# Attention on one core: the four column groups of the output moved within SBUF by SyncE and added by GpSimd, in place of eight matmuls and a VectorE copy

## The reference

```
q = (h @ Wq).reshape(Bb, Ss, H, Dh)
k = (h @ Wk).reshape(Bb, Ss, H, Dh)
v = (h @ Wv).reshape(Bb, Ss, H, Dh)
scores = jnp.einsum('bqhd,bkhd->bhqk', q, k) / jnp.sqrt(jnp.float32(Dh))
attn = jax.nn.softmax(scores, axis=-1)
ctx = jnp.einsum('bhqk,bkhd->bqhd', attn, v).reshape(Bb, Ss, Dd)
x = x + ctx @ Wo
```

## Time and profile before

| | |
|---|---|
| median of 3 runs | 3923.48 us (3914.27 to 3926.55) |
| span of the profiled execution | 3920.8 us, one core, mean granted clock 0.937 |
| PE busy | 3528.2 us (90%) |
| DVE busy | 2914.5 us (74%) |
| ACT busy | 2613.0 us (67%) |
| POOL busy | 696.1 us (18%) |

### The profile page before, as it was taken

One profiled execution on the slowest core, in us unless ns is written; L12 is line 12 of the kernel. 1 busy time (PEld: TensorE's weight loads), 2 busy tenths in 40 slices (PEclk: granted clock), 3 DMA queues, 4 the chain that ended last, 5 costly groups with the idle time before them and its releaser, 6 DMA issues. The chain is left out here.

```text
span 3920.8 us, 87382 instructions
## 1 busy us (share of the span) xinstructions
PE 3528.2 (90%) x29108; PEld 1918.7 (49%) x29108; DVE 2914.5 (74%) x5522; ACT 2613.0 (67%) x3037; POOL 696.1 (18%) x703
## 2 busy tenths in 40 slices
PE   8477999999999999999999999999999706999990
PEld 4243444444444444444444444444444605999980
DVE  1636999999999999999999999999996522333335
ACT  2132888888888888888888888888888103555540
POOL 0000000000000000000000000000000357888856
PEclk8595999999999999999999999999999757999995
DMA  3242010101101011010101101011000623444424
GB/s 95 81 161 51 12 25 14 24 13 26 24 13 26 13 24 25 13 24 13 26 16 21 26 12 25 14 24 25 14 12 7 204 102 126 146 136 138 142 83 133
DMA packets 158897, 206.66 MB, mean 53 GB/s; under 512 B 50064, under 2 KB 123664, under 8 KB 153232
## 3 DMA queue, kind: packets, MB, share of 16 engines
q1 hardware_dynamic: 140128, 173.78, 16.5%
q0 software_dynamic: 6336, 16.79, 1.4%
q10 hardware_dynamic: 12144, 12.06, 0.9%
HBM read 134.59 MB, written 66.85 MB: 51 GB/s over the span
## 5 line engine op out<-in xcount | busy, mean ns | idle before, releaser
L742 ACT ACTIVATE probs<-s_ps 128x1024 f32<-128x1024 f32 x2048 | 2056.1, 1026 | 408.6 <-PE s_ps L661 380.2
L776 DVE TENSOR_REDUCE unit_max<-m_ps 128x1 f32<-128x512 f32 x3584 | 2250.1, 686 | 57.1 <-PE m_ps L653 56.9
L676 PE MATMUL o_ps<-probs,v_here 128*32 128x256 f32 (+1 forms) x15360 | 1282.8, 406 | 0.5 <-ACT probs L742 0.5
L661 PE MATMUL s_ps<-q_stage,k_ring 50*128 50x512 f32 x4096 | 1024.4, 493 | 0.5
L653 PE MATMUL m_ps<-k_ring,q_stage 48*128 48x512 f32 x3840 | 963.6, 421 | 46.8 <-DMA q_stage<-qs_dram 25.9
L661 PEld LDWEIGHTS s_ps<-q_stage,k_ring 50*128 50x128 f32 x4096 | 384.2, 184 | 765.1 <-issue 646.2
L653 PEld LDWEIGHTS m_ps<-k_ring,q_stage 48*128 48x128 f32 x3840 | 619.9, 187 | 163.6 <-DVE unit_max L776 134.1
L676 PEld LDWEIGHTS o_ps<-probs,v_here 128*32 128x32 f32 x15360 | 303.2, 108 | 505.7 <-issue 502.7
L597 POOL TENSOR_TENSOR neg_max<-no_max,tile_max 128x4 f32<-128x4 f32 x127 | 25.3, 199 | 2447.9 <-DVE tile_max L791 2447.9
L1509 DVE TENSOR_TENSOR hidden_low<-h_ps,hidden_high 128x512 fp32r<-128x512 f32 x184 | 127.3, 692 | 366.4 <-ACT hidden_high L1473 366.4
L1469 ACT ACTIVATE h_ps<-h_ps,b_here 128x512 f32<-128x512 f32 x184 | 121.4, 660 | 255.4 <-PE h_ps L1406 255.4
(11 more groups left out here) (184 smaller groups left out, 2433.2 us busy)
## 6 DMA issues: line engine op xcount, KB each, us to landing
w_in<-in_W SPq DMA_DIRECT2D x46, 1024.0 KB, 4.9
q_stage<-max_turned SPq DMA_DIRECT2D x2048, 0.5 KB
q_stage<-qs_dram SPq DMA_DIRECT2D x768, 32.0 KB, 1.9
k_ring<-ks_dram SPq DMA_DIRECT2D x96, 128.0 KB, 4.3
slots_dram<-zero_rows SPq DMA_DIRECT2D x24, 512.0 KB, 6.7
rows_e<-slots_dram SPq DMA_DIRECT2D x24, 512.0 KB, 3.9
y_slots_dram<-y_out ACTq DMA_DIRECT2D x23, 512.0 KB, 4.3
qs_dram<-parts SPq DMA_DIRECT2D x16, 512.0 KB, 2.7
```

What stands on the lines that cost most here:

```text
L661: last = nc.tensor.matmul(s_ps[:, t % 2, k, :], k_ring[at:at + AROWS, par, P * t:P * t + P], q_stage[at:at + AROWS, buf * CHUNK:buf * CHUN ...
L676: last = nc.tensor.matmul(o_ps[at:at + SQ, lo:hi], v_here[:, par, first_tile(t) + 2 * k, :], probs[:, t, k, lo:hi], start=(pair == 0), sto ...
L742: nc.scalar.activation(probs[:, t, :, :], s_ps[:, t % 2, :, :], ACT.Exp).then_inc(exp_done, 1)
L776: nc.vector.tensor_reduce(unit_max[:, b, qt, 2 * j + k:2 * j + k + 1], m_ps[:, block_of(t, k) % 3, :], AX.X, ALU.max).then_inc(m_read, 1 + ...
```

## The change

`gather`, its making, `turn_o` and `copy_ctx` are gone. SP gets `align`: once `o_here` of chunk n is copied, it moves the three upper groups (17 partitions x 512 columns) with three transfers within SBUF to partitions 0 to 16 of `o_groups`. POOL gets `sum_o`: when all three have landed and the last store has read `ctx_stage`, it adds the four groups in three adds of 17x512 into `ctx_stage`, now 17x512 and single. SP's `store` is two transfers in place of five, one chunk later than before. In a chunk SP does `store(i - 2)` and then `align(i - 1)`, behind `rows(i + 1)` and `load_head`. POOL's list alternates `split_max(i + 2)` and `sum_o(i)`. ACT's `copy_o` also waits until the sum before last is done. The place of `turn_o` in the order of `m_ps` stays empty: DVE counts it off with the pair of slot 10, and PE's `block_of` is as it was.

```
@@ -470,7 +470,6 @@
         k_ring = sb("k_ring", [TOP_ROW + AROWS, 2, SIDE], F32R)
...
-        gather = sb("gather", [P, SQ])
@@ -480,14 +479,14 @@
...
         max_turned = sb("max_turned", [P, MROWS, SQ])
         o_here = sb("o_here", [P, CHUNK])
-        ctx_stage = sb("ctx_stage", [P, 2, P])
+        o_groups = sb("o_groups", [O_COLS, P // SQ - 1, CHUNK])
+        ctx_stage = sb("ctx_stage", [O_COLS, CHUNK])
@@ -527,21 +526,26 @@
...
-            def store(n, b, h, qc):
-                sp.wait_ge(m_read, n * RING_BLOCKS + ((LEAD + 1) * RING_BLOCKS + TURN_BLOCK + 1))
-                for t in range(TPC):
-                    sp.dma_start(dram["ctx"][ds(qc, 1), ds(h, 1), :, P * t:P * t + P].rearrange("a b c x -> (a b c) x"),
-                                 ctx_stage[SQ * t:SQ * t + DH, b, :]).then_inc(ctx_out[b], 16)
-                sp.dma_start(dram["z"][ds(h * CHUNKS + qc, 1), :].rearrange("a (t x) -> (a t) x", t=TPC),
-                             ctx_stage[DH:P:SQ, b, :]).then_inc(ctx_out[b], 16)
-
+            def align(n):
+
+                sp.wait_ge(o_copied, n + 1)
+                for g in range(1, P // SQ):
+                    sp.dma_start(o_groups[:, g - 1, :], o_here[SQ * g:SQ * g + O_COLS, :]).then_inc(o_aligned, 16)
+
+            def store(n, h, qc):
+                sp.wait_ge(o_summed, n + 2)
+                sp.dma_start(dram["ctx"][ds(qc, 1), ds(h, 1), :, :].rearrange("a b c x -> (a b c) x"),
+                             ctx_stage[0:DH, :]).then_inc(ctx_out, 16)
+                sp.dma_start(dram["z"][ds(h * CHUNKS + qc, 1), :], ctx_stage[DH:O_COLS, :]).then_inc(ctx_out, 16)
+
+            sp.sem_inc(ctx_out, 2 * 16)
...
-            def chunk(h, qc, loads=True, more=True, ahead=True, before=True):
@@ -552,37 +556,32 @@
                     rows(i + 1, (qc + 1) % Q_BUFS)
                 if more and qc == 0:
                     load_head(sp.snap(h + 1), sp.snap((h + 1) & 1))
-                if before:
-                    store(i - 1, 1 - qc % 2, sp.snap(h - 1) if qc == 0 else h, (qc - 1) % CHUNKS)
+                if before >= 2:
+                    store(i - 2, sp.snap(h - 1) if qc < 2 else h, (qc - 2) % CHUNKS)
+                if before >= 1:
+                    align(i - 1)
 
...
-            store(RING - 1, 1, sp.snap(HEADS - 1), CHUNKS - 1)
-            for b in range(2):
-                sp.wait_ge(ctx_out[b], 16 * (TPC + 1) * (RING // 2))
+            store(RING - 2, sp.snap(HEADS - 1), CHUNKS - 2)
+            align(RING - 1)
+            store(RING - 1, sp.snap(HEADS - 1), CHUNKS - 1)
+            sp.wait_ge(ctx_out, 2 * 16 * (RING + 1))
...
         @block.gpsimd
...
             nc.gpsimd.memset(v_here[:, :, :, :], 0.0).then_inc(v_consts, 1)
-            nc.gpsimd.memset(gather[:, :], 0.0).then_inc(v_consts, 1)
+            pool.wait_ge(v_consts, 1)
+            nc.gpsimd.memset(v_here[:, :, :, DH:O_COLS], 1.0).then_inc(v_consts, 1)
             pool.wait_ge(v_consts, 2)
-            nc.gpsimd.memset(v_here[:, :, :, DH:O_COLS], 1.0).then_inc(v_consts, 1)
-            nc.gpsimd.tensor_tensor(gather[:, 0:O_COLS], ident[:, 0:O_COLS], ident[:, SQ:SQ + O_COLS], ALU.add
-                                    ).then_inc(gather_chain, 1)
-            for n in range(2, P // SQ):
-                pool.wait_ge(gather_chain, n - 1)
-                nc.gpsimd.tensor_tensor(gather[:, 0:O_COLS], gather[:, 0:O_COLS], ident[:, SQ * n:SQ * n + O_COLS], ALU.add
-                                        ).then_inc(gather_chain, 1)
-            pool.wait_ge(gather_chain, P // SQ - 1)
-            pool.wait_ge(v_consts, 3)
-            pool.sem_inc(gather_ready, 1)
+            pool.sem_inc(o_summed, 1)
@@ -600,9 +599,21 @@
...
-            def split_maxima(lo, hi):
+            def sum_o(n):
+
+                pool.wait_ge(o_aligned, n * (16 * (P // SQ - 1)) + 16 * (P // SQ - 1))
+                pool.wait_ge(ctx_out, n * (2 * 16) + 2 * 16)
+                nc.gpsimd.tensor_tensor(ctx_stage[:, :], o_here[0:O_COLS, :], o_groups[:, 0, :], ALU.add).then_inc(o_added, 1)
+                pool.wait_ge(o_added, n * 2 + 1)
+                nc.gpsimd.tensor_tensor(ctx_stage[:, :], ctx_stage[:, :], o_groups[:, 1, :], ALU.add).then_inc(o_added, 1)
+                pool.wait_ge(o_added, n * 2 + 2)
+                nc.gpsimd.tensor_tensor(ctx_stage[:, :], ctx_stage[:, :], o_groups[:, 2, :], ALU.add).then_inc(o_summed, 1)
+
+            def split_and_sum(lo, hi):
+
                 with pool.Fori(lo, hi) as i:
-                    split_max(i + 1)
+                    split_max(i + 2)
+                    sum_o(i)
...
-            split_maxima(0, CHUNKS + 1)
+            split_max(pool.snap(1))
+            split_and_sum(0, CHUNKS - 1)
+            split_max(pool.snap(CHUNKS + 1))
@@ -621,15 +634,20 @@
                     pool.wait_ge(pv_done, (h + 1) * (CHUNKS * len(VISITS)))
                     pool.sem_inc(pool_passed, 1)
                     copy_v(h + 2, par)
-                    with pool.Fori(1, CHUNKS + 1) as qc:
-                        split_max(pool.snap((h + 1) * CHUNKS + qc + 1))
+                    sum_o(pool.snap((h + 1) * CHUNKS - 1))
+                    with pool.Fori(0, CHUNKS - 1) as qc:
+                        i = pool.snap((h + 1) * CHUNKS + qc)
+                        split_max(i + 2)
+                        sum_o(i)
+                    split_max(pool.snap((h + 2) * CHUNKS + 1))
                 ch.leave(HEADS // 2 - 1)
-            split_maxima((HEADS - 1) * CHUNKS + 1, RING - 1)
+            sum_o(pool.snap((HEADS - 1) * CHUNKS - 1))
+            split_and_sum((HEADS - 1) * CHUNKS, RING - 2)
+            for n in (RING - 2, RING - 1):
+                sum_o(pool.snap(n))
@@ -678,15 +696,6 @@
...
-            def turn_o(it, c):
-
-                pe.wait_ge(o_copied, it * PAIR + c)
-                pe.wait_ge(m_read, it * (PAIR * RING_BLOCKS) + ((c + LEAD) * RING_BLOCKS + TURN_BLOCK - 2))
-                for t in range(TPC):
-                    last = nc.tensor.matmul(m_ps[SQ * t:SQ * t + SQ, TURN_BLOCK % 3, 0:P], gather[:, :],
-                                            o_here[:, P * t:P * t + P], start=True, stop=True)
-                last.then_inc(o_turned, 1)
...
-                    if t == TURN_SLOT and c > 0:
-                        turn_o(it, c)
...
-            turn_o(HEADS // 2 - 1, PAIR)
@@ -730,6 +736,7 @@
 
             def copy_o(i):
                 act.wait_ge(pv_done, i * len(VISITS))
+                act.wait_ge(o_summed, i)
                 nc.scalar.activation(o_here[:, :], o_ps[:, :], ACT.Copy).then_inc(o_copied, 1)
@@ -776,14 +783,6 @@
...
-            def copy_ctx(i, b, stores):
-
-                dve.wait_ge(o_turned, i)
-                if stores is not None:
-                    dve.wait_ge(ctx_out[b], stores * (16 * (TPC + 1)))
-                nc.vector.tensor_scalar(ctx_stage[:, b, :], m_ps[:, TURN_BLOCK % 3, 0:P], 1.0, None, ALU.mult
-                                        ).then_inc(m_read, 1)
...
-            def chunk(n, b, ahead=True, finish=True, turn=True, stores=None):
+            def chunk(n, b, ahead=True, finish=True):
 
                 for t in range(UNITS):
                     if ahead:
-                        pair(n, t, b, 1 if t == TURN_SLOT and not turn else 0)
-                    if t == TURN_SLOT and turn:
-                        if not ahead:
-                            dve.wait_ge(m_read, n * RING_BLOCKS)
-                            dve.sem_inc(m_read, TURN_BLOCK)
-                        copy_ctx(n - LEAD, 1 - b, stores)
-                        if not ahead:
-                            dve.wait_ge(m_read, n * RING_BLOCKS + TURN_BLOCK + 1)
-                            dve.sem_inc(m_read, RING_BLOCKS - 1 - TURN_BLOCK)
+                        pair(n, t, b, 1 if t == TURN_SLOT else 0)
                     if finish and not ahead and t == FINISH_SLOTS[0]:
                         dve.wait_ge(rows_in, (RING - 1) * ROW_DMAS)
                     if finish and t in FINISH_SLOTS:
                         finish_max(n - 1, 1 - b, FINISH_SLOTS.index(t))
 
...
+            chunk(0, 0, finish=False)
+            chunk(1, 1)
+            with dve.Fori(1, RING // 2) as it:
                 for b in range(2):
-                    chunk(dve.snap(it * 2 + b), b, stores=it + (b - 2))
-            chunk(RING, 0, ahead=False, stores=RING // 2 - 2)
-            chunk(RING + 1, 1, ahead=False, finish=False, stores=RING // 2 - 1)
-            chunk(RING + 2, 0, ahead=False, finish=False, stores=RING // 2 - 1)
+                    chunk(dve.snap(it * 2 + b), b)
+            chunk(RING, 0, ahead=False)
```

18 lines of the change are left out of this document (5 added, 13 removed).

## The result

The changed kernel takes 4481.79 us (median of 4 runs, 4473.97 to 4486.97) beside 3922.87 us (3914.27 to 3926.55) for the kernel before: 1.144 times as long, with a 95% interval of 1.1414 to 1.1457. That is slower, and inside the range given; it is 210 us above the central value of 4272 us. The span of the profiled execution is 4480.4 us, 559.6 us more than before.

What follows compares the result with a forecast made beforehand. It took a PE-DVE turn of 20.96 us per chunk to bound the old kernel, a 22.85 us ring the new: 3923.5 + 236 (ring) + 105 (head chunks) + 8 (stage end) = 4272 us, range 3950 to 4530 us.

Steps and rivals of the forecast that it cites:

- the ring: Dependences from one DVE transpose through rows, stores, aligned transfers, adds and split to the next: 22.85 us, against 20.96 us per chunk.
- its upper end: Long case: each aligned transfer costs its full 2.7 us one after another, ring 24.9 us, 4530 us in all.
- The landing: Three 17-row transfers within SBUF, first issue to last landing: 6.05 us taken, 3.1 us at the low end.
- One engine: Each 17-row aligned transfer runs on one DMA engine, giving the 22.85 us ring; chance 0.74 with chunks ring-bound.
- rival 1: Aligned transfers spread over engines like `q_stage`'s: ring 19.9 us, head chunks 5.1 us late each, 3957 us; chance 0.13.
- Adds: GpSimd's three 17x512 adds in `sum_o`: 1.27 us each, 3.97 us with the gaps between them.
- The "faster" rival: GpSimd's add costs by its 17 rows, down to 0.224 us, with transfers spread and not queued: 3898 us; chance 0.05.
- Head chunks: In 14 chunks SP's nine next-head loads delay store by 5.0 us and aligned rows by 2.5 us more: 105 us.
- The end of the stage: From the last `o_here` to the next stage's first load: 13.0 us in place of 4.7 us, 8 us more.
- Waits that hold nothing up: ACT's `copy_o` waits for a sum that ends about six slots ahead; SP's `align` waits for a copy two slots early.
- rival 3: Adds or transfers slower than any row used, or PE losing its clock in head chunks: over 4530 us; chance 0.08.
- The gain on PE: Removing `turn_o` frees 0.33 us of PE in each of 127 chunks, 42 us, worth nothing while the ring is longer.

Runs made afterwards that it cites:

- the mended versions: Changed kernel with 32-row aligned transfers and a head's loads behind the aligned rows, 3917.0 us; the same with the split also ahead of the sum, 3919.7 us.
- the profiled run: Kernel before plus four constant VectorE reductions ahead of each transpose, slowest of four runs: 1.21 times the kernel before; median 4675.7 us.

## Why the prediction was right, and where it was not

The sign and the ring are right by their mechanism. That the time lies inside the range is in part luck: its upper end was worked out for slower transfers, and what lifts the time 210 us above the central value is PE's clock, which the sum did not have.

**The ring.** Right in kind and nearly in size: 22.85 us were worked out, 22.53 us measured; DVE's transpose waits mostly 1.6 to 2.0 us (about 2.2 us given), though in 80 of the turns and not in nearly every one: behind a turn with a low clock it often waits for nothing. Three terms were off. The stores cost 0.83 us and not 1.41 us, since the two transfers take 0.35 and 0.25 us to issue; a price by the piece from the old, cut-up transfers was too high. The landing took 6.76 us and not 6.05 us, which with the stores nearly cancels. The split and the hand-over took 0.65 us and not 0.98 us; the 0.35 us beyond the split had no row. 125 x 1.59 = 199 us, for 236 us.

**One engine.** The choice between the bounds was made by the issue times and by 17 rows dividing into nothing, and it carried the size, though not the sign: the kernel with 32 rows is rival 1 built, and it is slower too, at 4156.0 us where the rival's price was 3957 us. Its head chunks cost 7.2 us each and not 5.1 us, and the clock behind them 148 us that the rival had at nothing. The runs with 17 and 32 rows show the choice by themselves. The Trainium skill (DMA: Bandwidth & Descriptors, "Why a DMA increments its semaphore by 16 and not by 1") gives the rule behind it: the number of engines is the largest up to 16 that divides the slowest dimension of both sides, here the row count; by that rule 17 gives 1 and 32 gives 16, and the traces agree, with 6.76 and 3.45 us and with the engines' share of 0.04 to 0.07 and 0.53.

**Adds.** 1.27 us each, as measured, priced per element of a row and not per partition. The "faster" rival, that 17 rows make a short sum, fell with it.

**Head chunks.** 7.5 us each on top of the ring, 30.35 us per turn; measured 30.24 us. The two parts, SP's issues and queueing behind the loads' data, are both in the trace (9.4 us of landing in place of 6.76 us). What was wrong is the reading that I drew from it after the result, that their order on SP makes the difference: the run with the loads behind the aligned rows shows that a slow single-engine transfer is caught by the loads from either side. The end of the stage is right as well: from the last `o_here` to the next stage's first load it takes 7.9 us more, for 8 us.

**Waits that hold nothing up.** "ACT's `copy_o` ... about six slots ahead" is right for an ordinary chunk, and the changed kernel shows no wait there. It had no row for a chunk with a head's loads, and it is that chunk in which the copy becomes the late one once the ring is cut.

**The missing term.** The step that failed is the line "The ring repeats 125 times ... x (22.85 - 20.96)": it takes a chunk that waits at one place to be longer by its wait alone. PE's clock stands in the prediction in rival 3 only, for head chunks, where PE would idle over 5 us, and there with no price but "over 4530 us". The clock cost 237 us in all, more than the ring's own 199 us. Some 76 us of it are what rival 3 named, the turns behind the long waits. The larger part, some 164 us, comes from the short waits of ordinary chunks, 0.5 to 1.3 us each, which nothing in the prediction has. Without the clock the sum is 3923 + 199 + 108 + 15 = 4245 us, 27 us below the prediction; with 237 us for the clock it is 4482 us, as measured (it has to be: the terms are the split of the profiled execution). The trace of before has no row for it, since the only wait of PE in a turn is the one at slot 10. It could have been a rival of its own: the ring's waiting in every chunk was in the prediction, and that it would reach PE too.

**The gain on PE.** 0.12 us per turn, and not 0.33 us; it did not matter here, since the ring was longer, but it is what keeps the mended versions at 3917 to 3920 us and not near 3890 us.

## What to carry to other kernels

Moving work from a full engine to idle ones pays only if every new dependence ends before its consumer also in the worst chunk; find the closed ring (transpose, rows, stores, aligned rows, adds, split, transpose) and add it up before counting what was freed. Count the rows of a transfer: 32 rows of which 15 are waste landed in half the time of 17. And when a full PE is made to wait at all, price the clock beside the wait: 0.39 us per chunk cost the clock in few places, 0.98 us per chunk cost 4.6 us per chunk on top in the profiled run (578 us in 125), and some 3.4 us by the estimate above.
